# A two-layer graph network on one core: direct edges ahead of the upper half, degree and node-maximum products in one block each

## The reference, cut to what matters

```
h     = relu(layernorm(x))
e     = relu([h[src], h[dst]] @ W_kind + b_kind)      # kinds hh, oo, ho
logit = e @ W_a + b_a
ex    = exp(logit - segment_max(logit, dst)[dst]);  den = segment_sum(ex, dst)
z     = segment_sum((ex / den[dst])[:, None] * h[src], dst)
x     = x + relu([h, z] @ W_hn/W_on + b)              # first 128 nodes W_hn, the others W_on
h     = relu(layernorm(x))
c     = w / sqrt(w_out[src] * w_in[dst]), scaled by the degrees of both ends
x     = x + relu(segment_sum(c * h[src], dst) @ W + b)
```

## Time and profile before

| | us |
|---|---|
| median of 3 runs | 594.69 |
| the three runs | 589.58, 594.69, 595.25 |
| profiled execution, its own time | 592.03 |
| its span | 590.1 |
| TensorE busy in the span | 547.6 (93%) |
| VectorE busy | 417.7 (71%) |
| ScalarE busy | 218.9 (37%) |
| GpSimd busy | 162.8 (28%) |
| mean granted clock | 0.960 |

### The profile page before, as it was taken

The page is one execution under the profiler, slowest core; times in us unless marked ns, Lnnn a source line. Parts: engine busy times, 40 slices in busy tenths (PEclk is TensorE's granted clock), DMA queues, the critical chain, the costliest instruction groups (busy, mean ns, idle before and its releaser), DMA issues.

```text
span 590.1 us, 7545 instructions
## 1 busy us (share of the span) xinstructions
PE 547.6 (93%) x2489; PEld 360.2 (61%) x2489; DVE 417.7 (71%) x736; ACT 218.9 (37%) x291; POOL 162.8 (28%) x163
## 2 busy tenths in 40 slices
PE   2899999999999999897899996898888999989996
PEld 2788888544444444443454464876656888868885
DVE  6999632597798889897769486746975276877234
ACT  3522445899466360020102741012534163315200
POOL 4012140477656635564564100000000001121000
PEclk9999999999999999999899995759998999999999
DMA  8956891899999999999999933040001856104002
GB/s 334 380 223 214 280 361 78 283 409 410 410 411 414 410 408 412 412 409 410 409 409 409 369 108 108 4 144 1 3 2 26 295 170 197 62 0 143 0 37 107
DMA packets 42660, 142.69 MB, mean 242 GB/s; under 512 B 5216, under 2 KB 5408, under 8 KB 42624
## 3 DMA queue, kind: packets, MB, share of 16 engines
q1 hardware_dynamic: 22000, 69.22, 31.7%
q0 software_dynamic: 19136, 69.22, 29.9%
q10 hardware_dynamic: 1488, 3.78, 1.7%
HBM read 129.60 MB, written 12.60 MB: 241 GB/s over the span
## 4 chain that ended last, share of the span: by engine, by line
PE 78%; DVE 9%; DMA 6%; issue 3%; ACT 1%; DVEq 1%; POOL 1%; ACTq 0%
PE banks L1161 24%; PE banks L1122 23%; PE banks L1211 8%; PE banks L1310 7%; PE banks L1241 6%; PE banks L1327 4%; PE banks L1259 3%; DMA w_raw<-in_L_gnn_W_on_dram 3%; DMA w_raw<-in_L_gnn_W_hn_dram 3%; DVE masked L828 1%; DVE stats L694 1%; PE banks L1275 1%; PE banks L1150 1%; PE banks L1193 1%; DVE xf L1037 1%
## 5 line engine op out<-in xcount | busy, mean ns | idle before, releaser
L452 POOL DMA_INDIRECT rows<-table,ids_i x124 | 134.3, 1083 | 136.5 <-DVE rows L793 55.1
L1161 PE MATMUL banks<-w_raw,fT_raw 128*128 128x512 f32 x384 | 166.4, 593 | 4.4 <-DMA w_raw<-in_L_gnn_W_hn_dram 2.8
L1161 PEld LDWEIGHTS banks<-w_raw,fT_raw 128*128 128x128 f32 x384 | 72.5, 190 | 96.3 <-issue 87.8
L792 DVE TENSOR_TENSOR rows<-rows 128x1024 f32<-128x1024 f32 x62 | 75.9, 1224 | 35.2 <-DMA rows<-table,ids_i 34.7
L1122 PE MATMUL banks<-w_hi,fT_hi 128*128 128x512 f32 x200 | 77.9, 389 | 0.9 <-DVE fT_lo L746 0.9
L704 DVE TENSOR_TENSOR w_lo<-w_raw,w_hi 128x1024 fp32r<-128x1024 f32 x40 | 48.2, 1221 | 41.9 <-ACT w_hi L501 41.1
L1122 PE MATMUL banks<-w_hi,fT_lo 128*128 128x512 f32 x200 | 77.8, 389 | 0.0
L1122 PE MATMUL banks<-w_lo,fT_hi 128*128 128x512 f32 x200 | 77.8, 389 | 0.0
L793 DVE SCALAR_TENSOR_TENSOR rows<-rows,wa_rep 128x1024 f32<-128x1024 f32 x62 | 75.9, 1225 | 2.1
L501 ACT ACTIVATE w_hi<-w_raw 128x1024 fp32r<-128x1024 f32 x40 | 41.5, 1055 | 78.1 <-PE banks L1122 66.3
L1241 PE MATMUL banks<-pick_src,pick_dst 128*120 x158 | 51.1, 456 | 11.6 <-DVE span_end L880 8.3
(11 more groups left out here) (169 smaller groups left out, 661.6 us busy)
## 6 DMA issues: line engine op xcount, KB each, us to landing
w_raw<-in_L_gnn_W_ho_dram SPq DMA_DIRECT2D x16, 512.0 KB, 6.4
table<-stage SPq DMA_DIRECT2D x32, 256.0 KB, 6.5
w_raw<-in_L_gnn_W_oo_dram SPq DMA_DIRECT2D x16, 512.0 KB, 7.0
w_raw<-in_L_gnn_W_on_dram SPq DMA_DIRECT2D x16, 512.0 KB, 6.4
w_raw<-in_L_gnn_W_hn_dram SPq DMA_DIRECT2D x16, 512.0 KB, 6.2
w_raw<-in_L_gnn_W_hh_dram SPq DMA_DIRECT2D x16, 512.0 KB, 6.8
w_raw<-in_L_gnn_W_dram SPq DMA_DIRECT2D x8, 512.0 KB, 4.4
xf<-in_x_dram SPq DMA_DIRECT2D x4, 512.0 KB, 5.1
```

What stands on the lines that cost most here:

```text
L452: pool.indirect_dma_start(out=rows[:, slot, side, :], out_offset=None, in_=table[kind][side], in_offset=bass.IndirectOffsetOnAxis(ap=ids_i ...
L792: step(dve.tensor_tensor(rows[:, r, 0, :], rows[:, r, 0, :], rows[:, r, 1, :], ALU.add))
L1161: ins = pe.matmul(bank[j][:, :], fT_raw[:, k, m * P:(m + 1) * P], w_raw[:, c % SLOTS, n * H:(n + 1) * H], start=(k == 0), stop=(k == K - 1))
```

## The change

Direct edges run right behind unit 3, then the upper half. The upper half is turned round: `W_hn` on banks 0 and 1 first, then `W_on` on banks 4, 5, 6, 7, 2, 3. Direct edges use banks 4 to 7 for products, and banks 0 to 3 and then 0 and 1 for transposes; their transposed rows are written back into `h_edge` in place. `hh_edges` moves in VectorE's order from step 63 to step 51, ahead of edge tile 46. The value loads stand behind the first transposes. `spread(0)` moves behind the last edge tile and writes over `rows`, `spread(1)` writes over `fT_raw` and waits for the end of the upper half. All 256 degree products stand behind span 1, all node-maximum products behind span 6; the last `chunk_max` and `maxima` stand behind `spread(5)`, `exponents` behind `spread(8)`, `split3` behind `spread(10)`.

```diff
-    C_TOP = K * UNITS
-    C_HH = C_TOP + 2 * K
-    C_BOT = C_HH + 2 * K
+    C_HH = K * UNITS
+    C_TOP = C_HH + 2 * K
+    C_BOT = C_TOP + 2 * K
...
+        h_edge, early_at = sb("h_edge", [P, 2, TILE_HH, D], F32)
-        pick_src, _ = sb("pick_src", [P, T, N], BF16, over=fT_at)
+        pick_src, _ = sb("pick_src", [P, T, N], BF16, over=early_at)
...
-        pick_dst = [... for r, base in enumerate((tail, at))]
+        pick_dst = [... for r, base in enumerate((tail, fT_at))]
...
+        LAST_TOP = (4, 5, 6, 7, 2, 3)
-        BY_PE = {3: (C_TOP + 4, 0), 4: (C_TOP + K + 4, 6), 5: (C_HH + 4, 6), 6: (C_HH + 13, 4)}
-        LAST_MAX, ME_PE, ME_DVE, PARTS, EXP = 4, 4, 6, 8, 4
+        BY_PE = {3: (C_HH + 3, 2), 4: (C_HH + 10, 2), 5: (C_TOP + K, 0), 6: (C_TOP + K + 4, 0)}
+        HH_BANK = 4
+        LAST_MAX, ME_PE, ME_DVE, PARTS, EXP = 5, range(6, 7), 8, 10, 7
+        DEG_PE = (1,)
...
                 if pair < T // 8:
-                    act.wait_ge(chunk_used, C_HH + K + pair + 1)
+                    act.wait_ge(hh_logits, TILE_HH)
...
-                sp, slot = n % SPANS, (n + 1) % 2
+                sp, slot = n % SPANS, n % 2
+                if n == 1:
+                    dve.wait_ge(chunk_used, C_BOT)
...
-                if c == C_BOT - 1:
+                if c == 51:
                     hh_edges()
-                    dve.wait_ge(hh_logits, TILE_HH)
-                    spread(0, w_col)
...
+            transpose_edges(0)
             pe.wait_ge(words_ready, 1)
             words = [pe.value_load(...) for q in range(WORDS)]
-            transpose_edges(0)
...
+            for k in range(K):
+                raw_chunk(C_TOP + k, k, range(2), None)
+            pe.wait_ge(hh_logits, TILE_HH)
+            pe.wait_ge(max_done, B * 5)
+            for k in range(K):
+                raw_chunk(C_TOP + K + k, k, LAST_TOP, None)
+                spread_lifts(C_TOP + K + k)
...
-            pe.wait_ge(hh_raw_done, K)
-            pe.wait_ge(src_made, EARLY_SRC)
-            pe.wait_ge(max_done, B * 6)
-            degrees(range(T // 4, T), opens=True)
-            pe.wait_ge(max_done, B * 7)
             pe.wait_ge(src_made, T // 2)
             for n in range(2 * SPANS):
                 add_span(n)
                 if n:
                     fold_span(n - 1)
-                if n == ME_PE:
-                    degrees(range(T // 4), closes=True)
-                if n == ME_PE:
-                    node_maxima()
+                if n in DEG_PE:
+                    part = DEG_PE.index(n)
+                    degrees(range(T), part == 0, part == len(DEG_PE) - 1)
+                if n in ME_PE:
+                    node_maxima(ME_PE.index(n))
```

More of the change, by code:

```diff
@@ L88, in chunk_rows @@
             q, k = (c - (C_BOT if bottom else C_TOP)) // K, c % K
-            w, row = (W_hn if bool(q) != bottom else W_on), bottom * D + k * P
+            w, row = (W_on if q else W_hn), bottom * D + k * P
         else:
@@ L144, in build @@
         tail = rows_at + ROWS * 2 * D * 4 - 2 * B * N * 4
-        pick_dst = [sb(f"pick_dst{r}", [P, T, 3, SPAN], BF16, over=base)[0] for r, base in enumerate((tail, at))]
+        pick_dst = [sb(f"pick_dst{r}", [P, T, 3, SPAN], BF16, over=base)[0] for r, base in enumerate((tail, fT_at))]
         wa_rep, at = sb("wa_rep", [P, D], F32)
@@ L255, in bank_ready @@
             elif unit == TOP:
-                if j in (1, 7):
-                    eng.wait_ge(chunk_used, first + (2 * K if j == 1 else K))
+                if j in (1, LAST_TOP[-1]):
+                    eng.wait_ge(chunk_used, first + (K if j == 1 else 2 * K))
                 else:
-                    eng.wait_ge(bank_done, before + (j - 1 if j > 1 else 6))
+                    eng.wait_ge(bank_done, before + (2 + LAST_TOP.index(j) if j else 1))
             elif j == (3 if unit == HH else 7):
@@ L384, in _ @@
                 for c in range(K * (u + 1) + (SLOTS if u else LEAD), K * (u + 2) + SLOTS):
-                    if c < C_TOP + SLOTS:
+                    if c < C_HH + SLOTS:
                         load(c)
-            for c in range(C_TOP + SLOTS, C_HH + SLOTS):
-                load(c)
             for c in range(C_HH + SLOTS, C_BOT + SLOTS):
@@ L552, in keep_edges @@
                     act.wait_ge(hhT_ready, side * (K // 2) + g + 1)
-                    act.activation(fT_raw[:, 2 * g:2 * g + 2, side * 2 * P:(side + 1) * 2 * P],
-                                   bank[4 + g % 2].rearrange("p (f e) -> p f e", f=2), ACT.Copy).then_inc(hh_raw_done, 1)
+                    act.activation(h_edge[:, side, :, 2 * g * P:2 * (g + 1) * P],
+                                   bank[g % 2 if side else g].rearrange("p (f e) -> p f e", f=2), ACT.Copy).then_inc(hh_raw_done, 1)
             def pick(n):
@@ L952, in exponents @@
                 dve.tensor_tensor(me[:, :], rest[:, :], lb[:, :], ALU.subtract).then_inc(arg_ready, 1)
-            for n in range(1, SPANS):
+            for n in range(SPANS):
                 spread(n, w_col)
@@ L1152, in spread_lifts, with raw_chunk @@
                         ins.then_inc(lift_full, 1)
-            def raw_chunk(c, k, banks, evac_wait=8 * UNITS - 8):
+            def raw_chunk(c, k, banks, evac_wait):
                 pe.wait_ge(w_in[c % SLOTS], 16 * (c // SLOTS + 1))
                 for j in banks:
-                    if k == 0:
+                    if k == 0 and evac_wait is not None:
                         pe.wait_ge(evac, evac_wait + j + 1)
@@ L1210, in _ @@
                     r, n = j // 2, j % 2
-                    ins = pe.matmul(bank[j][:, :], fT_raw[:, k % K, (2 * side + r) * P:(2 * side + r + 1) * P],
+                    if k == 0:
+                        pe.wait_ge(evac, 8 * UNITS - 8 + HH_BANK + j + 1)
+                    ins = pe.matmul(bank[HH_BANK + j][:, :],
+                                    h_edge[:, side, k % 2, (k % K // 2 * 2 + r) * P:(k % K // 2 * 2 + r + 1) * P],
                                     w_raw[:, c % SLOTS, n * H:(n + 1) * H], start=(k == 0), stop=(k == 2 * K - 1))
@@ L1268, in fold_span, with node_maxima @@
                               start=True, stop=True).then_inc(rows_summed, 1)
-            def node_maxima():
+            def node_maxima(part):
                 pe.wait_ge(mpart_ready, 1)
-                for t in range(T):
+                for t in range(part * T // len(ME_PE), (part + 1) * T // len(ME_PE)):
                     for b in range(B):
```

66 lines of the change are left out of this document (28 added, 38 removed).

## The result

The changed kernel takes 596.18 us (median of 14 runs, 591.04 to 599.34) against 591.7 us for the kernel before, measured beside it (589.28 to 596.71). The ratio is 1.0065, interval 1.004 to 1.009: slower by 0.65%, 3.9 us (the two medians lie 4.5 apart). Times are medians of all runs of a kernel; ratios and their 95% intervals leave out executions in a slower state that every kernel shows now and then. The forecast was 588.5, some 3.5 us faster. The profiled execution of the changed kernel took 596.38 us, 4.35 more than that of before.

A forecast was written before the change was run, and what follows sets the result against it. TensorE holds 78% of the chain of waits, so time is won only where it stands or runs at lower clock. 0.1 + 2.7 - 4.3 - 2.0 = -3.5 us from 592.03 gives 588.5; forecast 583 to 592 (0.48), range 581 to 597.

The forecast's parts named there:

- Dense products: From 215.85 us: transposes -1.3, value loads -0.6, weights +2.0; sum 0.1 us, ending at 347.1.
- The rule that transposes don't count as busy: Behind unit 3: transposes and value loads would halve the clock for first direct products, 1.7 us worse; nothing added.
- VectorE: Beside the dense products: `spread(0)` at 340.6 without gather waits, taken as 344, leaving 3 us of cover.
- rival 2: VectorE becomes the bound ahead of span 0 through late gathers: span 0 at 352.8, +4.7 us or 597; chance 0.16.
- The degree block: Behind span 1: 256 products take 6.9 us, same cost as before, end 358.4; spans 2 and 3 at half clock.
- rival 1: Clock stays up through degree block and node maxima: spans 2 and 3 end 361.8, -13.8 us or 578; chance 0.08.
- The stand ahead of span 6: `spread(6)` waits behind `spread(5)` and 6.3 us of `chunk_max` and `maxima`: span 6 starts at 375.9.
- the terms 2.7 - 4.3: Span 7 at 385.9, 2.7 us later than span 5 before (383.19), with two more spans done, -4.3 us.
- Half clock behind the maxima: Behind the node maxima: 12 us at half clock in place of 15.9, -2.0 us.
- The later spans, features and layer two stay as they are: Behind span 7 and the half clock there: no change in time claimed.
- rival 3: Weights are late: ten direct chunks lose 3.5 us, two-matmul chunks 3.4 us more; 595, no change; chance 0.14.
- The fourth: Clock falls in the stand at span 6, stays down 16 us after the maxima: about 0, 592; chance 0.14.

The follow-up runs named there:

- number 8: Changed kernel with the seven value loads spread, one behind each of direct chunks 8 to 14: 595.99 us, ratio 1.0063 to the kernel before.
- number 11: Changed kernel with late bias loads, both blocks behind span 4 with maxima at 4, and value loads spread: 586.77 us, ratio 0.9879 to the kernel before.
- the square: Ratios to the kernel before, new order; degree products 192 and 64: 0.9897 (maxima at 4), 0.9960 (at 6); all 256 behind span 1: 0.9993, 1.0065.
- number 1: Changed kernel with degree products (192 ahead of span 0, 64 behind span 4) and maxima put back, new order kept: 586.01 us, ratio 0.9897.
- number 2: Kernel before, old order of dense work, with only the degree products and maxima moved to their new places: 604.08 us, ratio 1.021.
- number 3: Changed kernel with maxima, node maxima, exponents and split put back to spans 4, 4, 6, 8; degree block stays behind span 1: 592.17 us, ratio 0.9993.
- number 5: Changed kernel with two bias loads moved behind the node maxima and the load of h: 593.72 us, ratio 0.9996 to the kernel before.
- number 6: Changed kernel without the 256 degree products: 585.22 us, ratio 0.985 to the kernel before.
- Number 9: Changed kernel with only the last chunk_max and maxima moved from behind spread 5 to behind spread 3: 589.23 us, ratio 0.9943 to the kernel before.
- number 7: Changed kernel with all degree products, then the node maxima, behind span 4; maxima, exponents, split at 4, 6, 8: 585.94 us, ratio 0.9858.
- number 4: Changed kernel with degree products put back (192 ahead of span 0, 64 behind span 4), maxima kept behind span 6: 590.06 us, ratio 0.996.

## Why the prediction was wrong, step by step

Of the 7.9 us between the forecast and the profiled execution (588.5, 596.38), 5.7 lie ahead of span 7 and 2.2 behind it.

**Dense products.** Forecast 347.1, measured 348.2, direct edges 283.5 and 283.3. (The sum's 0.1 us stands in it twice, since 385.9 is reckoned from 347.1.) Transposes cost 1.9 us (2.1). The value loads stood TensorE 3.04 us (2.24) and the 3.4 us behind them ran at half clock, 1.7 us more, which I had named with the transposes and added nothing for. The transposes alone don't do it: in number 8 the same transposes, without the loads behind them, are followed by full clock, and in number 11 half clock follows a wait of 3.9 us in the same part. The rule that transposes don't count as busy (the Trainium skill, "TensorE: Matmul & The Clock Gate", Part 4: PE-mode transpose) gave the right size here, 1.7 us, by luck: number 8 doesn't bear out its reason. The wait for `W_hh` (forecast 1.8) did not appear, since the late start hid it; the others, 4.4 us, were forecast as 4.6.

**VectorE.** Forecast: `spread(0)` ready at 344, 3 us of cover. Measured:

```profile
286.15 1.22 DVE L791 TENSOR_TENSOR rows<-rows 128x1024 f32<-128x1024 f32 x1
...
346.52 0.21 DVE L812 STREAM_TRANSPOSE liftT<-lifted 128x32 f32<-128x32 f32 x1
...
348.68 0.06 DVE L881 MEMSET span_end<- 128x1 bf16 x1
```

It went on at 286.15 as forecast (286.3), and was ready at 348.7, since 7.6 us of waits came on top of the 340.6 without any: 5.0 us for gathers, and 2.6 us ahead of one edge sum for which the profile names no releaser. That is rival 2 in small. It cost 1.0 us.

**The degree block: the step that failed.** "They cost the same as before, only in one block." They did not: the square gives 1.0% (6 us) for the block's place alone. I did not see that the 192 products ahead of span 0 were cover for `spread(0)`, and the 64 behind span 4 for the maxima (numbers 1, 2 and 3), nor the 2.0 us gap (number 5). The clock I had: the sum runs spans 2 and 3 at half clock, 365.2 against 361.8 in rival 1, and so holds 6.9 + 3.4 = 10.3 us for the block, where number 6 gives 12.7. On the time axis this made span 2 start at 362.78 and not at 358.4: 1.1 us from the dense products, 1.0 from `spread(0)` that nothing covered, 0.3 from the spans themselves, 2.0 from the gap.

**The stand ahead of span 6.** The mechanism was right and was named: forecast start 375.9, measured 380.52, and of these 4.6 us 4.4 are inherited from span 2. But its price was too low: span 6, a fold and the node maxima took 11.07 us, all at half clock, where I took 10. Number 9 shows 7 us for the stand and its half clock. With 391.59 in the place of 385.9, the terms 2.7 - 4.3 of the sum become 8.4 - 4.3: a loss of 4.1 us and not a gain of 1.6.

**Behind it.** Half clock behind the maxima was 3.3 us, not 12: that term becomes -6.3 in place of -2.0, and leaves 2.2 us of gain with the others. By span 11 these are spent: `split3`, now behind `spread(10)`, made a stand of 2.6 us there (1.15 before) that I had no term for, and small waits took the rest. "The later spans, features and layer two stay as they are" failed too: 4.3 us were lost behind span 11, most of them at half clock at 405, at 442.7 and at 527 us. The code there is the same and so is the wait ahead of 442; why the clock fell there stays open.

**Rivals.** The first (the clock stays up in a busy block) is refuted: 6.90 us busy of 6.90, clock 0.50. The advice of the Trainium skill ("TensorE: Matmul & The Clock Gate", "Why this matters for your kernels") to keep TensorE busy did not suffice. By number rivals 2 (597) and 3 (595) were nearest, by luck: gathers were late as rival 2 asks (5.0 us, over its 3), but made span 0 late by 1.0 us and not 5.7, and the weights were on time. The fourth, at 592, had the right stand, but not the half clock behind the maxima that it asks for. The change was two changes, an order that gains 1.0% and block places that lose 1.7%. I added them up along one time axis and never asked what each was worth alone; for the order alone, a forecast of faster would have been right.

## What to carry to other kernels

Small products that stand in front of a late producer are cover: before a block is moved, ask who waits behind its old place. Put blocks of tiny products where they lie over the other engine's longest serial piece (numbers 7 and 9). Putting them next to each other saves a fall of the clock too, but by one pair of traces that is worth only about 1 us here. And split a change into its parts on paper, with a price for each alone.

## What the runs showed of the hardware that I had not expected

- Seven value loads on TensorE in a row stand it 2.7 to 3.9 us (the changed kernel, numbers 1, 3 to 7, 9); spread behind direct chunks, no stand of theirs is seen (number 8).
- Half clock on dense span work lasts very differently: 3.3, 8.2, 15.9 and 16.3 us for the same kind of work. Behind the same wait of 1.9 us near 441 us, the clock stayed up in one kernel and fell for 6.9 us in the other. A forecast can only carry a range for it. Runs of one kernel differ in it too: the changed kernel took 591.04 us at a mean clock of 0.963 and 597.27 us at 0.947.
- A run of 256 short products can stop for 0.6 to 2.3 us at nearly the same product; it goes on 2.3 to 2.6 us after a code transfer begins, and the stop was gone with less on SP's queue (number 5).
